# Windowed attention and FFN on one core: another order of loads and weight splits ahead of the first scores

## The reference

```
x = x + attention(layernorm(x))        # 16 heads of 16, causal window of 64 keys, softmax, Wo
x = x + FFN(layernorm(x))              # relu(x @ T(W1).T + b1) @ T(W2).T + b2, 256 -> 1024 -> 256
T(W) = clip(round(W / (mean(|W|) + 1e-5)), -1, 1)
```

## Time and profile before

| | |
|---|---|
| median of 3 runs | 694.69 us (694.3 to 695.87) |
| the profiled execution's own time | 692.33 us |
| its span, first to last instruction | 690.4 us |
| busy share PE / DVE / ACT / POOL | 94% / 91% / 90% / 90% |
| granted clock, mean | 0.983 |

### The profile page before, as it was taken

One profiled execution on the slowest core, in us unless ns is written; L12 is line 12 of the kernel. 1 busy time (PEld: TensorE's weight loads), 2 busy tenths in 40 slices (PEclk: granted clock), 3 DMA queues, 4 the chain that ended last, 5 costly groups with the idle time before them and its releaser, 6 DMA issues.

```text
span 690.4 us, 24485 instructions
## 1 busy us (share of the span) xinstructions
PE 649.0 (94%) x8048; PEld 552.7 (80%) x8048; DVE 628.3 (91%) x1596; ACT 623.9 (90%) x2649; POOL 618.0 (90%) x869
## 2 busy tenths in 40 slices
PE   7668699999999999999999999999999999998887
PEld 5446488888888888888888888887888888887776
DVE  5779889999999999999999999999999999899864
ACT  5689899999999999999999999998999999898833
POOL 7388999999999999999999999999899999999930
PEclk9879989999999999999999999999999999999999
DMA  8576656465756656475756657475665646464000
GB/s 293 80 98 103 75 96 73 77 86 74 125 73 99 98 99 95 77 95 72 128 68 101 96 92 105 51 117 74 102 91 99 74 82 71 61 93 70 18 31 31
DMA packets 497988, 61.17 MB, mean 89 GB/s; under 512 B 470724, under 2 KB 493510, under 8 KB 497864
## 3 DMA queue, kind: packets, MB, share of 16 engines
q1 hardware_dynamic: 487160, 50.82, 51.2%
q10 hardware_dynamic: 10704, 8.80, 4.2%
HBM read 11.86 MB, written 8.39 MB: 29 GB/s over the span
## 4 chain that ended last, share of the span: by engine, by line
PE 40%; POOL 32%; issue 10%; ACT 9%; DVE 6%; DMA 1%; SPq 0%; POOLq 0%; DVEq 0%; ACTq 0%
POOL p L393 13%; POOL tl L417 10%; PE ps L1089 9%; PE ps L1077 7%; ACT p L496 6%; PE ps L987 5%; POOL th L411 5%; PE ps L967 5%; PE ps L1024 4%; PE ps L1035 3%; PE ps L1050 3%; ACT hTh L573 1%; PE ps L1062 1%; POOL rstdC L386 1%; PE ps L960 1%
## 5 line engine op out<-in xcount | busy, mean ns | idle before, releaser
L496 ACT ACTIVATE p<-ps,negm 128x96 f32<-128x96 f32 x1024 | 340.3, 375 | 8.4 <-DVE negm L711 7.7
L417 POOL TENSOR_TENSOR tl<-pt,th 128x384 f16<-128x384 f32 x256 | 234.6, 916 | 16.3 <-ACT th L505 1.8
L496 ACT ACTIVATION_READ_ACCUMULATOR p<-ps,negm 128x1 f32 x1024 | 248.5, 244 | 0.0
L393 POOL TENSOR_TENSOR p<-p,rden 128x384 f32<-128x384 f32 x256 | 214.3, 837 | 7.3 <-DVE rden L718 6.9
L724 DVE STREAM_TRANSPOSE pt<-p 128x384 f32<-128x384 f32 x256 | 141.5, 553 | 14.3 <-POOL p L393 12.9
L711 DVE TENSOR_REDUCE negm<-ps 128x4 f32<-128x384 f32 x256 | 136.0, 531 | 10.4 <-PE ps L967 8.1
L967 PE MATMUL ps<-k,qbd 128*128 128x96 f16 x1536 | 125.2, 208 | 0.0
L967 PEld LDWEIGHTS ps<-k,qbd 128*128 128x128 f16 x1536 | 106.0, 99 | 9.6
L987 PE MATMUL ps<-th,vb 128*128 128x96 f16 (+1 forms) x1120 | 97.1, 202 | 1.8 <-POOL tl L417 1.8
L1077 PE MATMUL ps<-xTCh,w1T 128*128 128x256 f16 x512 | 97.6, 272 | 0.8 <-ACT xTCh L568 0.8
L573 ACT ACTIVATE hTh<-ps 128x512 f16<-128x512 f32 x128 | 79.6, 623 | 19.9 <-PE ps L1077 19.7
(11 more groups left out here) (139 smaller groups left out, 1486.7 us busy)
## 6 DMA issues: line engine op xcount, KB each, us to landing
k<-kst SPq DMA_DIRECT2D x32, 288.0 KB, 4.1
vb<-vd SPq DMA_DIRECT2D x256, 32.0 KB, 2.6
out<-x SPq DMA_DIRECT2D x32, 256.0 KB, 2.5
qbd<-qs SPq DMA_DIRECT2D x254, 32.0 KB, 2.3
x<-in_L_attn_hidden ACTq DMA_DIRECT2D x15, 512.0 KB, 5.4
kw<-kst SPq DMA_DIRECT2D x31, 192.0 KB, 3.8
k<-kst SPq DMA_DIRECT2D x31, 144.0 KB, 3.4
vb<-in_L_ffn_W SPq DMA_DIRECT2D x2, 1024.0 KB, 7.6
```

The lines of the kernel that those rows point to most:

```text
L393: e.tensor_tensor(p3, p3, rden[n % 4][:, :].unsqueeze(2).to_broadcast([128, 4, 96]), ALU.mult).then_inc(s_nm, 1)
L417: e.tensor_tensor(tl[g % 2][:, o], pt[n % 3][:, :], th[g % 2][:, o], ALU.subtract).then_inc(s_lo, 1)
L496: ins = e.activation(p[:, 96 * u:96 * u + 96], bank[:, 96 * u:96 * u + 96], ACT.Exp, bias=m[:, u:u + 1], accum_out=r[:, u:u + 1])
```

## The change

- SP: kmask ahead of identf, smask behind Wq; Wk and Wv leave SP's queue and stand on ACT's, ahead of the load of chunk 1 and of Wo.
- Slot -16 prepares only Wq and Wk. Wv moves to slot -13 (PE) and -12 (ACT, DVE), Wo to slot -9 (PE) and -6 (ACT, DVE). Wv and Wo use banks 6 and 7. `a_t` waits for two low halves instead of six, `a_qk` of chunk 0 for four, `a_v` for six.
- The 8 and the 6 idle matmuls between the weights are gone; the first 28 stay.
- The load of chunk 2 moves from slot -16 to -6, behind Wo's high halves; `masks` from slot -16 to -12.
- Chunk 1: statistics in slots -7 and -6, rstd in slot -5, norm in slot 0, both halves. Those of the later chunks stay.
- `fold_consts` and `bias_low` move from slot -8 to slot 2, ahead of all else that DVE has there.

```diff
--- before.py
+++ after.py
@@ -21,7 +21,7 @@
 V_LATE = 11
 A_T, A_Q, A_K, A_V = (1, 2), (6, 14), (6, 15), (8, 12)
 A_STATS, A_RSTD, A_NORM = (-24, -16), -9, (-9, -8)
-N_STATS, N_RSTD, N_NORM = ((-16, 0, 10), (-15, 1, 16)), (-11, 5, 23), ((-3, 9, 23), (-1, 11, 24))
+N_STATS, N_RSTD, N_NORM = ((-7, 0, 10), (-6, 1, 16)), (-5, 5, 23), ((0, 9, 23), (0, 11, 24))
 Q_DMA, K_DMA, V_DMA, A_CARRY = (7, 20), (14, 19), 15, 1
 C_WO, C_STATS, C_RSTD, C_NORM = (7, 10), (8, 13), (10, 15), (10, 15)
 C_T, C_F, C_Y = (11, 16), (13, 19), (18, 24)
@@ -302,14 +302,12 @@
                 e.dma_start(out_t[c][:, 2 * u:2 * u + 2, :], xs[c % NX][:, 2 * u:2 * u + 2, :]).then_inc(d_out[c % 2], 16)
 
             e.dma_start(xs[0][:, 0:2, :], x_t[0][:, 0:2, :]).then_inc(d_x[0], 16)
+            e.dma_start(kmask, kmask_d).then_inc(d_km, 16)
             e.dma_start(identf[:, :], identf_d).then_inc(d_id, 16)
-            e.dma_start(kmask, kmask_d).then_inc(d_km, 16)
-            e.dma_start(smask, smask_d).then_inc(d_s, 16)
             for t in range(2):
                 e.dma_start(nat["q"][:, t, :], wq_d[128 * t:128 * t + 128].rearrange("(g r) d -> r g d", g=2)
                             ).then_inc(d_w["q"], 16)
-            for n, d in (("k", wk_d), ("v", wv_d)):
-                e.dma_start(nat[n], d.rearrange("(t p) d -> p t d", p=128)).then_inc(d_w[n], 16)
+            e.dma_start(smask, smask_d).then_inc(d_s, 16)
             e.dma_start(pr[1][:, :], maskf_d).then_inc(d_m, 16)
             e.wait_ge(s_bz, 1)
             for r in (0, 32):
@@ -471,7 +469,7 @@
                 for w in ws:
                     n, t = "qkvo"[w // 2], w % 2
                     e.wait_ge(s_wp, w + 1)
-                    e.activation(wT[n][0][:, t, :], banks[4 + w % 4][:, 0:256], ACT.Copy,
+                    e.activation(wT[n][0][:, t, :], banks[4 + w if w < 4 else 6 + w % 2][:, 0:256], ACT.Copy,
                                  scale=WS * (0.25 if n == "q" else 1.0)).then_inc(s_whi, 1)
 
             def magnitudes(j):
@@ -576,16 +574,19 @@
             for n in SLOTS:
                 if n == SLOTS[0]:
                     e.dma_start(xs[0][:, 2:4, :], x_t[0][:, 2:4, :]).then_inc(d_xb, 16)
+                    for w, d in (("k", wk_d), ("v", wv_d)):
+                        e.dma_start(nat[w], d.rearrange("(t p) d -> p t d", p=128)).then_inc(d_w[w], 16)
                     load_x(1)
                     e.dma_start(nat["o"], wo_d.rearrange("(t p) d -> p t d", p=128)).then_inc(d_w["o"], 16)
                     mask_keys()
                 if n == -16:
-                    weights(range(6))
-                    e.wait_ge(s_wlo, 4)
+                    weights(range(4))
+                if n == -12:
+                    weights(range(4, 6))
+                    masks()
+                if n == -6:
+                    weights(range(6, 8))
                     load_x(2)
-                    masks()
-                if n == -12:
-                    weights(range(6, 8))
 
                 if n == A_K[0] + 2 - 16:
                     place_q(e, 0, 0, ((), (), (0, 1)))
@@ -667,7 +668,7 @@
 
             def weights(ws):
                 for w in ws:
-                    n, t, bank = "qkvo"[w // 2], w % 2, banks[4 + w % 4]
+                    n, t, bank = "qkvo"[w // 2], w % 2, banks[4 + w if w < 4 else 6 + w % 2]
                     hi, lo, src = wT[n][0][:, t, :], wT[n][1][:, t, :], bank[:, 0:256]
                     e.wait_ge(s_whi, w + 1)
                     e.scalar_tensor_tensor(out=lo, in0=src, scalar=WS * (0.25 if n == "q" else 1.0), in1=hi,
@@ -824,10 +825,12 @@
                 if n == SLOTS[0]:
                     consts()
                 if n == -16:
-                    weights(range(6))
+                    weights(range(4))
                 if n == -12:
+                    weights(range(4, 6))
+                if n == -6:
                     weights(range(6, 8))
-                if n == -8:
+                if n == 2:
                     fold_consts()
                     bias_low()
                 if n == W_TERNARY[0] - 2:
@@ -891,10 +894,10 @@
         def _(e):
             def weights(ws):
                 for w in ws:
-                    n, t, bank = "qkvo"[w // 2], w % 2, banks[4 + w % 4]
+                    n, t, bank = "qkvo"[w // 2], w % 2, banks[4 + w if w < 4 else 6 + w % 2]
                     e.wait_ge(d_w[n], 32 if n == "q" else 16)
                     if w >= 4:
-                        e.wait_ge(s_wlo, w - 3)
+                        e.wait_ge(s_wlo, w - 1)
                     for c in range(2):
                         ins = e.transpose(bank[:, c * 128:(c + 1) * 128], nat[n][:, c, t * 128:(t + 1) * 128],
                                           identf[:, :])
@@ -993,7 +996,7 @@
                 if held is None and bank < 4:
                     return banks[bank]
                 if held is None and bank < 6:
-                    e.wait_ge(s_wlo, 6)
+                    e.wait_ge(s_wlo, 2)
                 elif held is None:
                     e.wait_ge(s_fe, 6)
                     e.wait_ge(s_td, 8)
@@ -1015,6 +1018,8 @@
 
             def a_qk(c, t, n):
                 bank = free("A", c, (2, 6)[t] + "qk".index(n))
+                if c == 0:
+                    e.wait_ge(s_wlo, 4)
                 e.wait_ge(s_ahi, 8 * c + 2)
                 m = 0
                 for wp, xp in PARTS:
@@ -1028,6 +1033,8 @@
 
             def a_v(c, u):
                 bank = free("A", c, 4 + u)
+                if c == 0:
+                    e.wait_ge(s_wlo, 6)
                 for t in range(2):
                     m = 0
                     for wp, xp in PARTS:
@@ -1102,10 +1109,9 @@
             for n in SLOTS:
                 if n == -16:
                     weights(range(4))
-                    idle(8)
+                if n == -13:
                     weights(range(4, 6))
-                    idle(6)
-                if n == -13:
+                if n == -9:
                     weights(range(6, 8))
                 if n == W_TERNARY[0] - 1:
                     mean()
```

## The result

The changed kernel is slower by a little: median 696.3 us of 20 runs against 694.15 of 20 runs of the kernel before, ratio 1.0037 with a 95% interval from 1.0023 to 1.0051, so 2.2 us by the medians and 2.6 by the ratio. The interval lies above 0.2%. The prediction was 694.6, no difference. The profiled execution took 695.52 us (span 693.8), 3.19 more than that of before.

A forecast was written before the change was run, and what follows sets the result against it. ACT's first exponential was taken to set the start of a work-bound stream. Gains of 1.8 us at q and 2.0 at statistics meet two new chains, exponential 2 at 34.8 against 34.85, so 694.6 us; range 692.2 to 696.9.

The forecast's parts named there:

- What bounds the kernel: From 37.68 us slots cost the sum of their work; a change ahead can only move the start of POOL's stream.
- Part 1, loads: Start of the kernel: Wq lands at 7.7, kmask at 5.4; kw ends at 8.3, xnA at 9.2 instead of 10.27.
- Part 2, xnA and q: PE's xnA transposes start at 10.35, 3.4 us sooner; q low and k high clock; q evicted at 15.7, before 17.53.
- First scores = q's eviction + 10.45: SP's ten q transfers, then PE's first scores: 15.7 + 10.45 = 26.15, 1.8 us sooner.
- Part 3, norm: Chunk 1's statistics and norm moved: DVE's xT path loses 2.0 us; first exponential at 28.9 against 29.28.
- V + 8.6: From V, ACT's first v eviction in slot -7 (20.3), through chunk 1's statistics and norm to first exponential: 8.6 us.
- the prediction's own signs of failing: Fails if clock reads 1.00 from 10 us, first exponential waits for other than chunk 1's norm, or DVE waits for x2.
- rival 4: Norm chain shorter, first exponential up to 1.4 us sooner, exponential 2 still fold-bound: 694.6; forecast with its first half 0.42.
- Part 4, fold: Fold constants in DVE's slot 2 take 3.76 us, 0.3 of it showing; exponential 2 at 34.8, before 34.85.
- Part 5, x2: Chunk 2's load issued at 21.5, lands at 26.9; DVE wants it at 27.9, so hidden by 1 us.
- Rival 3: x2 lands at 30.2, 2.3 us behind DVE's want, sent while SP's q transfers are under way: 696.9; chance 0.15.
- The sum: Gains of 1.8 and 2.0 us, and two new chains ending where the old one did: 34.8 against 34.85; time 694.6.

The follow-up runs named there:

- best1: e_head with fold constants in slot 0 and chunk 1's statistics in slots -12 and -11, rstd -8, norm -3 and -1; 692.15 us, ratio 0.9961.
- b_head: The kernel before with chunk 1's and Wo's loads issued behind the kw activations; 693.19 us, ratio 0.9989.
- e_head: a_x2_early with chunk 1's and Wo's loads issued behind the kw activations; 692.37 us, ratio 0.9968.
- a_x2_early: The changed kernel with chunk 2's load put back in slot -16, behind the high halves of Wq and Wk; 694.76 us, ratio 0.9997.
- e_norm_old: a_x2_early with statistics, rstd and norm of chunk 1 back in their old slots; 693.4 us, ratio 0.999.

## Why the prediction was wrong, point by point

**What bounds the kernel** held up to block 16: every kernel but those whose clock fell in slot 11 (best1, b_head, and e_head by a little) carried its offset from the start of POOL's stream to there within 0.1 us. Behind it the profiles drift by up to 2.1 us, in both directions. One part of that drift has a place: in seven of the fourteen profiles the clock falls to 0.50 at 631 to 634 us, and these seven lose 1.3 to 1.5 us between blocks 240 and 250; the other seven, among them the kernel before, lose nothing there (0.04 at most). So a front's gain is read at the stream's start, and the time shows it only as a median of many runs.

**Part 1, loads:** kmask landed by 4.68 (I took 5.4), kw ended at 7.54 (8.3) and xnA at 8.56 (9.2), all better. But kw began right behind ACT's table load (3.39 to 4.67 us), and kmask had landed at 4.4, so its landing no longer hid the two more loads that ACT issues, as I had said. Wq failed: 9.61, outside my bounds of 7.2 and 8.44. I counted what stood ahead of it on its own queue and let Wk and Wv, 0.5 MB, move to the other as if that were out of the way. Ahead of it and beside it the engines are full, 280 to 374 GB/s in every microsecond from 3 to 10; by the 350 of that stretch 0.5 MB are 1.5 us, and the flight grew by 1.64 (5.04 to 6.68). This is an estimate, and the move of Wk and Wv was not tried by itself; that holding back ACT's two later loads shortens the flight by 2.4 us is shown by e_head.

**Part 2, xnA and q:** the transposes began at 11.77, 1.4 later than forecast, behind Wq. The low clock came as forecast (0.50 from 8.7 to 15.6), q ran partly low, k high. q's eviction 16.50 against 15.7, k's 17.80 against 17.05: 0.8 off, since 1.4 us late at the first transpose and 0.6 quicker from there than my sum.

**First scores = q's eviction + 10.45:** this is the step that failed. I had the 10.45 from one row and carried it over as a constant, though it is ten DMAs long and another part of the same change puts half a megabyte beside the last two. It was 13.39; that is 2.94 of the 3.74 us by which the scores missed (29.89 against 26.15), the other 0.8 is q.

**Part 3, norm:** V + 8.6 to the first exponential was right where it can be seen. In a_x2_early V is 21.18, and ACT goes without a break from the norm of chunk 1 through magnitudes into the first exponential, V + 8.4:

```profile
26.55 2.08 ACT L511 ACTIVATE xnA<-x,shiftA,rstdA 128x256 f32<-128x256 f32 x4 [2.32 <-POOL shiftA L377]
28.54 1.04 ACT L478 ACTIVATE hTh<-vb 128x1024 f16<-128x1024 f32 x1
...
29.57 0.32 ACT L494 ACTIVATE p<-ps,negm 128x96 f32<-128x96 f32 x1
```

In the changed kernel V was 20.98 and magnitudes ended at 29.48, but the scores were later and decided, at 31.64: the first exponential waited for the scores and not for the norm of chunk 1, which was one of the prediction's own signs of failing. That the norm's chain costs nothing either way was rival 4, and e_norm_old bears it out.

**Part 4, fold:** 2.46 us (34.57 to 37.03), not 3.76; I carried the duration over from a place beside POOL's clearing, and the term was 1.3 us too large. The exposed wait of ACT ahead of exponential 2 is 0.31 us, as forecast, but the sum from scores to exponential 2 was 7.80, not 8.6: 1.3 less for the fold, and 0.46 more ahead of the first `biggest`, where the low clock over the first scores was not in my sum.

**Part 5, x2:** issued at 21.06 (I had 21.5), landed 7.4 us later, at 28.5, where I had 5.4 and had named 6.4 as the point from which it costs. DVE did not wait for it all the same: with the scores late it took its statistics only at 32.12. But that was the wrong question. Rival 3, the one that ends slower, had the right place, and its sentence even says that x2 slows SP's packets; I priced only x2's own landing, against DVE's want, and gave it 0.15. What x2 does to the others was in a sentence by itself, without a price and without a place in the chances.

**The sum:** forecast for exponential 2, 34.75; + 0.8 for q, + 2.94 for the transfers, - 0.8 from there to exponential 2 = 37.69, as measured. 696.3 lies within the range, but by luck: the upper end, 696.9, was the price of a wait of DVE for x2 that did not come.

## What to carry to other kernels

When a load is moved, price it twice: for who wants it, and for which transfers it then runs beside. A string of small DMAs that ends the critical path is not a constant; here its last ones more than doubled their landing beside one large load. Both queues feed the same 16 DMA engines (in the changed kernel's first 12 us they take 48.1% and 40.4% of the engines' time): Wk and Wv on the other queue did not bring Wq sooner (its flight grew from 5.04 to 6.68 us), two later loads issued after `kw` did (4.3 us). And where a front gets faster, read the granted clock behind each place where PE stands still: in three profiles here it fell in slot 11 and took back part or all of the gain, and the length of the wait there did not tell which.

## What I had not expected of the hardware

- A 32 KB `qbd` transfer landed in 2.3 us without chunk 2's load beside it, in 5.2 beside its 512 KB and in 3.7 beside half of them.
- DVE's f32 reads of identf took 0.22 to 0.28 us each where POOL cleared nothing and up to 2.80 beside its clearing of `vb`.
- With ten idle matmuls of 1.25 us in all, in the one gap of slot 11, the clock stayed at 1.00, and the stream was 1.6 us farther ahead at block 16 (2.5 against 0.9), by one profile of each kernel.
- The clock fell in slot 11 behind a wait of 1.20 us (e_head) and of 1.66 (b_head), and not behind one of 1.76 (the kernel before).
